# Output products in two PSUM banks from the second tile, and a new order of the last tiles' value product, roundings and scales

## The reference

```
x = x + xattn(layernorm(x), ctx)
x = x + ffn(layernorm(x))

bit_linear(x, w, b):
    scale_x = 127 / max(|x|) per token
    x_q = round(x * scale_x) / scale_x
    w_q = clip(round(w / mean|w|), -1, 1) * mean|w|
    return x_q @ w_q.T + b

ffn(x): bit_linear(silu(bit_linear(x, gate)) * bit_linear(x, val), out)     # hidden size 1024
```

## Time and profile before

| what | value |
|---|---|
| median of 3 runs | 61.09 us (60.72 to 61.1) |
| the profiled execution | 60.99 us |
| its span, first to last instruction | 59.3 us |
| PE busy | 51.3 us, 87% of the span |
| VectorE busy | 48.2 us, 81% |
| ScalarE busy | 47.6 us, 80% |
| GpSimd busy | 44.9 us, 76% |
| granted TensorE clock, mean | 1.000 of full speed |

### The profile page before, as it was taken

How to read it: one execution, slowest core, us unless ns; L and a number is a source line. 1 busy time by engine, 2 the same in 40 slices (tenths; PEclk the granted TensorE clock), 3 DMA queues, 4 the chain that set the end, 5 groups by cost and what they waited for, 6 DMA issues and landing times.

```text
span 59.3 us, 1140 instructions
## 1 busy us (share of the span) xinstructions
PE 51.3 (87%) x298; PEld 32.7 (55%) x301; DVE 48.2 (81%) x122; ACT 47.6 (80%) x84; POOL 44.9 (76%) x102
## 2 busy tenths in 40 slices
PE   1999998899999699929899988899999997979910
PEld 1768866468888478613323634333473752759800
DVE  3249859897999799996998989898999997997150
ACT  0723929989999999979999685999999999798700
POOL 4970002798789888798779978989999999999900
DMA  0789999999993000000002001299270199920573
GB/s 0 161 232 369 409 339 409 408 407 411 397 400 136 0 17 0 0 6 0 6 0 44 0 0 32 57 180 174 51 137 0 31 185 178 242 72 0 176 235 120
DMA packets 11070, 8.92 MB, mean 150 GB/s; under 512 B 7605, under 2 KB 9141, under 8 KB 11065
## 3 DMA queue, kind: packets, MB, share of 16 engines
q1 hardware_dynamic: 10912, 8.72, 47.5%
q10 hardware_dynamic: 152, 0.14, 1.3%
HBM read 6.04 MB, written 1.05 MB: 120 GB/s over the span
## 4 chain that ended last, share of the span: by engine, by line
POOL 30%; PE 26%; issue 17%; DVE 12%; ACT 9%; POOLq 0%; ACTq 0%
POOL h L344 6%; PE psO L940 5%; PE psT L753 5%; POOL r_cols L276 4%; PE psV L763 3%; DVE nmax L467 3%; PE psG L763 3%; PE psH L940 3%; PE psT L778 3%; POOL rstd L311 3%; ACT o_early L723 3%; DVE x L485 3%; POOL pgam L325 2%; POOL res L372 2%; POOL w_int L409 2%
## 5 line engine op out<-in xcount | busy, mean ns | idle before, releaser
L572 DVE TENSOR_REDUCE pmax<-prod 128x1 f32<-128x1024 f32 x8 | 9.7, 1210 | 0.1
L707 ACT ACTIVATE sil<-psG,s_gv 128x1024 f32<-128x1024 f32 x8 | 8.9, 1112 | 0.6 <-PE psG L874 0.2
L556 DVE TENSOR_TENSOR prod<-psV,sil 128x1024 f32<-128x1024 f32 x7 | 8.5, 1221 | 0.9 <-ACT sil L707 0.5
L859 PE MATMUL psG<-ter_gate,hT 128*128 128x512 bf16 x31 | 8.0, 378 | 0.8 <-ACT sil L707 0.7
L886 PE MATMUL psV<-ter_val,hT 128*128 128x512 bf16 x26 | 7.0, 381 | 0.2 <-issue 0.2
L940 PE MATMUL psO<-ter_out,pT 128*128 128x256 bf16 x48 | 6.2, 273 | 0.7 <-ACT o_early L723 0.7
L940 PEld LDWEIGHTS psO<-ter_out,pT 128*128 128x128 bf16 x48 | 4.4, 98 | 2.4 <-DVE pT L599 0.8
L281 POOL TENSOR_SCALAR ve<-mv 128x2 f32<-128x2 f32 (+1 forms) x3 | 0.6, 197 | 6.0 <-DVE mv L463 5.9
L694 ACT ACTIVATE hT<-psH,unshift 128x256 bf16<-128x256 f16 x8 | 3.8, 475 | 1.5 <-PE psH L842 1.4
L859 PEld LDWEIGHTS psG<-ter_gate,hT 128*128 128x128 bf16 x32 | 2.7, 96 | 4.0 <-issue 2.0
L644 ACT ACTIVATE prob<-psT,nmax 128x256 f32<-128x256 f32 x8 | 3.7, 479 | 1.1 <-DVE nmax L467 1.1
(11 more groups left out here) (142 smaller groups left out, 144.9 us busy)
## 6 DMA issues: line engine op xcount, KB each, us to landing
w_gate<-in_w_gate SPq DMA_DIRECT2D x2, 512.0 KB, 5.1
x<-in_x_tok SPq DMA_DIRECT2D x4, 256.0 KB, 6.3
w_val<-in_w_val SPq DMA_DIRECT2D x2, 512.0 KB, 7.2
xt_sb<-in_x_T SPq DMA_DIRECT2D x4, 256.0 KB, 7.8
w_out<-in_w_out SPq DMA_DIRECT2D x2, 512.0 KB, 8.9
out_x<-res SPq DMA_DIRECT2D x8, 128.0 KB, 1.8
ctx_sb<-in_ctx_T SPq DMA_DIRECT2D x2, 128.0 KB, 2.8
ctx_sb<-in_ctx_T SPq DMA_DIRECT2D x1, 256.0 KB, 6.0
```

Source lines behind the costliest of these rows:

```text
L556: nc.vector.tensor_tensor(prod[:, t % P_RING, :], psV[:], sil[:, t % S_RING, :], ALU.mult).then_inc(prod_done, 1)
L572: nc.vector.tensor_reduce(pmax[:, t:t + 1], prod[:, t % P_RING, :], AX.X, ALU.max, apply_absolute_value=True).then_inc(pmax_done, 1)
L707: nc.scalar.activation(sil[:, t % S_RING, :], psG[:], ACT.Silu, scale=s_gv[:, t, 0:1]).then_inc(sil_done, 1)
L859: nc.tensor.matmul(psG[:, c * HC:(c + 1) * HC], hT[:, t, k, :], w_ter[0][:, k * HID + c * HC:k * HID + (c + 1) * HC], start=(k == 0), stop ...
```

## The change

The core of the diff, with all five lists that it touches:

```diff
-        ALT = 5
+        ALT = 1
         ps_o = [psH[:, 0:D] if t >= ALT and t % 2 else psO[:, 0:D] for t in range(T)]
...
 (GpSimd)
-            add_bias_shift(5); gamma_p(4); p_round_int(3); scale_out(1); add_residual(0); scale_out(2);
-            add_bias_shift(6); scale_out(3); gamma_p(6); add_residual(1); p_round(6); add_bias_shift(7);
-            scale_out(4); scale_out(5); add_residual(2); add_residual(3); add_residual(4); scale_out(6);
-            scale_out(7)
+            add_bias_shift(5); gamma_p(4); p_round_int(3); scale_out(1); p_round_int(5); scale_out(2);
+            add_bias_shift(6); add_residual(0); scale_out(3); p_round(6); scale_out(4); scale_out(5);
+            scale_out(6); add_bias_shift(7); add_residual(1); add_residual(2); scale_out(7); add_residual(3);
+            add_residual(4)
...
 (VectorE)
-            invert_gamma_p(5); times_value(6); p_max(6); widen(3); invert_gamma_p(6); times_value_half(0);
-            times_value_half(1); p_max(7); gamma_p(7); invert_gamma_p(7); p_round_half(1); p_copy(6);
-            add_residual(5); add_residual(6); add_residual(7)
+            invert_gamma_p(5); times_value(6); p_max(6); gamma_p(6); invert_gamma_p(6); widen(3);
+            times_value_half(0); times_value_half(1); p_max(7); gamma_p(7); invert_gamma_p(7); p_round_half(0);
+            p_copy(6); add_residual(5); add_residual(6); add_residual(7)
...
 (ScalarE)
-            silu(6); p_round_int(4); scale_product(1); p_round_int(5); silu(7); scale_product(2); widen(4);
-            scale_product(3); widen(5); p_round_half(0); scale_product(4); p_copy_half(0); p_copy_half(1)
+            silu(6); p_round_int(4); scale_product(1); silu(7); scale_product(2); widen(4); scale_product(3);
+            widen(5); p_round_half(1); scale_product(4); p_copy_half(0); p_copy_half(1)
...
 (TensorE)
-            gate(6); biases(6); value(6); last_product(1); gate(7); biases(7); last_product(2); value(7);
+            gate(6); biases(6); value(6); last_product(1); gate(7); biases(7); value(7); last_product(2);
             last_product(3); p_transpose(6); last_product(4); last_product(5); p_transpose_half(0);
             p_transpose_half(1); last_product(6); last_product(7)
```

## The result

The changed kernel takes 62.48 us in the median of 4 runs (62.01 to 62.7) against 61.06 for the kernel before. The ratio is 1.0257, with a 95% interval of 1.0209 to 1.0305. The forecast was 62.4. The profiled execution took 62.34 us with a span of 60.6, so 1.35 more than the 60.99 before, and again 1.7 lie around the span. All medians here are of all executions, while the ratios come from the fast executions alone (for the kernel before, 13 of 22 beside experiments 1 to 4 and 10 of 33 beside 5 to 8), so a ratio there can differ by up to 0.8% from that of the two medians printed beside it.

A forecast was written before the change was run, and what follows sets the result against it. GpSimd's full queue was taken to bound the kernel, its fifth `add_residual` holding store 4 and those behind it. The sum was 60.99 + 1.42 (last store later) + 0 (all else) = 62.4 us, range 61.4 to 62.9.

The forecast's parts named there:

- The rounding on GpSimd: `p_round_int(5)` on GpSimd adds 1.09 us and, starting at 46.70, a wait of 0.23 for tile 5's `pqs`.
- The end of GpSimd's queue: GpSimd's full queue hands on all added work: fifth `add_residual` ends at 57.3 in place of 55.66.
- The contention: VectorE's cast and half rounding slow GpSimd beside them by 0.22 and 0.27 us; bounds neither (56.8) and twice (57.8).
- The stores: Stores 5 to 7 queue behind store 4 on SyncE, 0.39 a step; store 7 at 58.51 for 57.09, +1.42 us.
- VectorE, "nothing to -0.2 us": `gamma_p(6)` moved to VectorE fits where it idled 0.27 us ahead of `widen(3)`: net nothing to -0.2 us.
- PE's pause of 1 us: With product 3 right behind product 2, PE idles about 1 us from product 3's end until the transposes.
- Another sign: The changed trace should show ScalarE idle before `widen(4)` for longer than 0.49 us.
- Two banks, value first, halves swapped: Output banks, `value(7)` ahead of product 2, swapped half roundings: 0 on the path; bounds for the banks 0 and -0.2.
- A: Rival: GpSimd's backlog isn't felt, store 4 isn't late, and `silu(7)`'s 0.49 us may reach the end: 60.5; chance 0.10.
- B: Rival: smaller backlog, no contention with VectorE, issues 0.35 apart: 61.8, or 61.6 without the 0.23 wait; chance 0.14.
- C: Rival: the four last stores collide and landing grows from 1.8 us to 2.1 or beyond: 62.9 to 63.2; chance 0.07.
- D: Rival: TensorE's clock falls to 1.2 GHz after PE idles 1 us before the transposes: 65.4 in all; chance 0.03.

The follow-up runs named there:

- experiment 1: Changed kernel with only `p_round_int(5)` put back on ScalarE: 61.59 us, ratio 1.0156 to the kernel before.
- experiment 2: Changed kernel with only SyncE's store list reordered to tiles 0, 5, 1, 2, 6, 3, 7, 4: 61.48 us, ratio 1.0099 to the kernel before.
- experiment 3: Kernel before with only `p_round_int(5)` moved from ScalarE to GpSimd, behind `scale_out(1)`: 62.08 us, ratio 1.0168.
- experiment 4: Kernel before with only the two output banks from tile 1 on: 61.02 us, ratio 1.0010.
- experiment 5: Changed kernel with `p_round_int(5)` back on ScalarE and `add_residual(1)` ahead of `p_round(6)` on GpSimd: 61.08 us, ratio 0.9990 to the kernel before.
- experiment 6: Changed kernel with GpSimd's list of before (without `gamma_p(6)`) and `p_round_int(5)` on ScalarE: 61.08 us, ratio 1.0038 to the kernel before.
- experiment 7: Changed kernel with the stores of tiles 5, 6 and 7 issued by ScalarE at its list's end: 61.35 us, ratio 1.0141 to the kernel before.
- experiment 8: The kernel of experiment 6 with the stores of tiles 5 to 7 issued by ScalarE: 61.29 us, ratio 1.0118 to the kernel before.
- experiment 9: Changed kernel with `scale_out(3)` ahead of `add_residual(0)` on GpSimd: 62.64 us, ratio 1.0292 to the kernel before.

## Why the prediction was right, point by point

*The rounding on GpSimd, +1.09 and a wait of 0.23.* Measured: 1.12 and 0.20, its successor 1.10 later (46.48 to 47.58). Right. The "about 0.1 for the semaphore" had no row behind it; here it was 0.09 (`pqs` done at 46.39, start at 46.48).

*The end of GpSimd's queue.* Forecast 57.3, which is 12.47 behind the anchor; measured 12.41. The full queue did hand on what was put into it.

*The contention.* Its sum was nearly right (0.41 us for 0.49), its place half wrong. I had `add_residual(0)` stretched by the cast; it ran in 0.72, and the cast waited for it. GpSimd paid at the next scale instead (0.52 for 0.34) and, beside the half rounding, at `add_bias_shift(7)` (0.71 for 0.48): 0.18 and 0.23 against the 0.22 and 0.27 of the forecast. By the rule of the Trainium skill ("GPSIMD Engine Reference", Specifications) the interface is shared. These rows agree in that each side is stretched beside the other; which mode VectorE ran in, no row shows. The measured 12.41 fits the forecast with both stretches (12.47), not the 11.97 without them (56.8 - 44.83).

*The stores.* Forecast +1.42, measured +1.51 (12.26 to 13.77). The term that was too small is the step between issues: 0.39 forecast, (58.38 - 57.04) / 3 = 0.45 measured, within the bounds given. Experiments 2 and 7 show that the delay is this queue. That the medians differ by exactly the forecast's 1.42 (62.48 - 61.06) is partly luck: the profiled ones differ by 1.35, since the tail is 1.51 longer and the part ahead of the anchor was 0.22 shorter.

*VectorE, "nothing to -0.2 us".* This step failed. The half products of tile 7 start at 5.48 (50.09 - 44.61) for 5.05 before: 0.43 later, because the cast moved under a two-input add of GpSimd. It cost nothing in the time; experiment 9 takes it away and the time stays. For the same reason product 3 was not right behind product 2, and PE's pause of 1 us came as two of 0.38 and 0.30. Another sign was off too: the 0.76 us of ScalarE's idle time stood ahead of the reading of product 2, not of `widen(4)`.

*Two banks, value first, halves swapped: 0.* Experiments 4, 5 and 6 agree: 1.0010, 0.9990 and 1.0038. VectorE's last add was forecast to stay and came 0.15 later.

*The rivals.* A falls: nothing of the gain of `silu(7)` (0.5 us) reaches the last product, and the backlog was real. B would have given 61.6 to 61.8; the contention was there and the issues were slower, not faster. C: the landing stayed at 1.7 to 1.9 us in a row of four. D: the clock stayed at 1.00 (2.4 GHz), but the pause of 1 us that it rested on did not come. Experiment 3 had one of 1.65 us, and there too the clock stayed at 1.00. By the rule of the Trainium skill ("TensorE: Matmul & The Clock Gate", What's actually happening), that the gate follows how busy the array has lately been, it could have fallen. The trace agrees with it only behind the last matmul, which ends at 56.47: from 59 us to the span's end at 60.6 the mean granted clock is 0.74, when nobody waits for TensorE any more.

*What I had not split* is the loss into its two causes. I booked the whole on the moved rounding, and expected experiment 1 to give it all back. Reordering was said to cost GpSimd nothing in sum; that holds only while the queue has no wait. Once the rounding is gone it has one of 0.47.

## What to carry to other kernels

An engine with a full queue can be a bound even where the chain of waits names others, and where its busy share is the lowest of all (GpSimd's 76%): read its order of time, find which of its last results somebody in another queue waits for, and count all work put in ahead of that one at full price. In an ordered store queue the slowest tile's store sets when all behind it go, so either the stores stand in the order in which tiles end, or a tile's last step is not left to the engine whose queue ends last. Taking load from an engine that then waits for a DMA or a product (ScalarE here) was worth nothing.

## What the runs showed of the hardware

- A VectorE cast from int16 to bf16 (0.43 us) and a two-input GpSimd add (0.72 us) hardly run side by side, and the one that starts second is stretched. Cast first by 0.08, the add took 0.92; add first by 0.01, the cast took 0.99; add first by 0.34, the cast took 0.68 (experiment 5, 48.97 and 49.31). In all three the stretch (0.20, 0.56, 0.25) is 0.14 or 0.15 less than what was left of the first one when the second started (0.35, 0.71, 0.39).
- A half rounding of 0.49 took up to 0.93 (experiment 8) beside such adds.
- Issues of stores of 128 KB on SyncE's queue take 0.33 us alone and 0.43 to 0.46 right behind another store (changed kernel and experiment 2), and the first one behind the transposes took 0.49 in the changed kernel and 0.58 before; the landing took 1.7 to 1.9 us either way in the changed kernel. What lengthens the issue isn't shown.
- The granted clock stayed at 1.00 through a pause of PE of 1.65 us (experiment 3). In the changed kernel it was 1.00 until 59 us and 0.74 on the mean from there to 60.6, with no matmul since 56.47.
